# Scores of 192 columns a head pair in place of 256, and the routing's one-hot matrices written by VectorE alone

## The chip, the cores and the metric

The program runs on one core of a Trainium2 chip. The metric is the device time of one execution in microseconds (us); the lower, the better. Engines are named as in the profile: PE (TensorE, with PEld for its weight loads), DVE (VectorE), ACT (ScalarE), POOL (GpSimd), SP (the queue that issues most transfers).

## What is computed

One layer of a small model over 2 x 512 tokens of 256 features, everything in f32: a retention attention and a mixture of experts, both on the layer-normalised input, summed with the residual.

```python
attn = einsum('bhid,bhjd->bhij', q, k) * SCALE            # 16 heads of 16 features
gammas = 1.0 - exp(linspace(log(1/32), log(1/64), H))
dist = arange(S)[:, None] - arange(S)[None, :]
scores = attn * gammas[:, None, None] ** abs(dist) * (dist >= 0)
y = layernorm(einsum('bhij,bhjd->bhid', scores, v)) ; attention = (y * silu(x @ wg.T)) @ wo.T
top_vals, top_idx = top_k(xf @ router_w.T + router_b, 4)   # 32 experts, 4 for each token
rw = softmax(top_vals) * 1.8
routed = sum over the 4 experts of rw * ((silu(x gate_w.T) * (x up_w.T)) @ down_w.T)
shared = (silu(x shared_gate_w.T) * (x shared_up_w.T)) @ shared_down_w.T
out = x + attention + routed + shared
```

## The kernel before

The 1024 tokens are eight tiles of 128 (t = 0 to 7), four to a sequence. Attention goes tile by tile: inside a tile by scores, between tiles by a running state (`from_state`, `chunk_products`, `update_state`). Each engine has its own list of steps in program order, written out by hand, and engines wait for each other by semaphores only. PE's list sets the pace: for each t it has `scores(t)`, transposes of keys and outputs, the projections of tile t+1 (`project_qk`, `project_vg`), `transpose_back(t-2)`, `from_state(t)`, `project_out(t-2)`, `weigh_values(t)`. An output goes through seven hands: PE `weigh_values`, ACT copy, PE transpose, DVE `output_moments`, POOL `output_scale` (four small operations), ACT `normalise_output`, then `gate_output` (three operations of 128 x 256, on POOL or, for tiles 2, 5, 6 and 7, on DVE), then PE `transpose_back` and `project_out`, and DVE `add_residual`. `transpose_keys` for the next tile waits for that residual, since both use one PSUM bank.

**Scores.** The 8 heads of a half g lie in 4 row groups of 32 features (r = 0 to 3), two heads (par = 0, 1) to a row group. ACT makes two copies of the queries with one head of each pair zeroed (`qeo`). One matmul per (g, r) has the 128 keys as weights and the 2 x 128 masked queries as moving columns, so a head pair has 256 columns of scores, of which a quarter (queries of the first 64, keys of the last 64) is zero by the causal mask. The four row groups go to four PSUM banks. DVE's `decay_scores(t, r)` multiplies 512 columns of each bank with the decay table; `weigh_values` multiplies with the values, 16 matmuls of 128 columns, each into its own group of 32 columns of the array.

**Routing.** While attention runs, the choices of experts become slots (`choose_slots`, `assign_slots` at t = 3), and from these two sets of one-hot matrices over 32 groups of choices (a): `pos_hot[a]` (128 x 128, the position in a block) and `blk_code[a]` (128 x 2 x 60, the block, once times a number for (t, k) and once times the token's number). The program makes `pos_hot` by subtraction on ACT (27 of the 32, as |position - column|, at places given by `HOT_STEPS`) and on POOL (`POOL_HOT`, 5 of them), and DVE compares the result with zero, 16 groups at a time (`one_hot_positions`, L1061). DVE makes `blk_hot` (L1064) and its first product (`code_blocks`, L1070), ACT the second (`code_rows`, L597). PE's `route_inverse` (L1422, 32 matmuls) stands behind `scores(6)`; its result becomes `codes` (`make_codes`), with which POOL gathers the tokens of each expert by indirect transfers (L830). The experts then go pair by pair (`transpose_pair` L1553, `gate_up` L1575, `down` L1589), 16 pairs, and the shared expert and the sums end the program.

Of the kernel before, what the change touches and what calls it, by code (L numbers as in the profile page):

```python
# [8 lines left out]
BF16 = mybir.dt.bfloat16  # L9
# [6 lines left out]
P = 128  # L16
# [36 lines left out]
POOL_HOT = range(5, 10)  # L53
HOT_STEPS = {(3, "y"): 5, (4, "z"): 6, (4, "rows"): 2, (5, "tok"): 1, (5, "qk"): 2, (5, "vg"): 11}
HOT_PARTS = 2
# [6 lines left out]
CT = 32  # L62

# [9 lines left out]
C_FILL = C_PI + 1  # L73
# [5 lines left out]


def head_of_slot(s):

    r, g, par = s // 4, s // 2 % 2, s % 2
    return HG * g + 2 * r + par


def constants():
# [13 lines left out]
    c[:, C_PI] = i  # L101
    c[:, C_FILL] = ROWS + P + i
# [7 lines left out]
    dist = i[None, :] - i[:, None]  # L110
    decay = np.zeros((P, H, P))
    for s in range(H):
        decay[:, s] = np.where(dist >= 0, SCALE * gammas[head_of_slot(s)] ** np.maximum(dist, 0), 0.0)
    return c.astype(np.float32), decay.reshape(P, H * P).astype(np.float32)
# [31 lines left out]
def build(nc, x, consts, decay, w_router, w_qkvg, w_out, lnwb, rbias, w_exp, w_late, w_ovf2, w_shared, xn_rows, xnt_rows, y_rows, out):  # L146
    with ExitStack() as ctx:
# [81 lines left out]
        dec = early(H * P)  # L229
        st = early(H * P)  # L230
        qeo = early(2, 2 * KT * P)
# [45 lines left out]
        blk_hot = xb_mem[:, 0:NA * NB // 2].bitcast(BF16).rearrange("p (a b) -> p a b", a=NA)  # L277
# [49 lines left out]
        q_ready = sem("q_ready")  # L327
# [133 lines left out]
        def _(sp):  # L461
# [11 lines left out]
            sp.dma_start(dec[:, 0:H * P // 2], decay[:, 0:H * P // 2]).then_inc(d_in, 16)  # L473
            sp.dma_start(dec[:, H * P // 2:H * P], decay[:, H * P // 2:H * P]).then_inc(c2_in, 16)
# [82 lines left out]
        def _(act):  # L557
# [23 lines left out]

            act_hot = [a for a in range(NA) if a not in POOL_HOT]
            hot = [0]

            def hot_positions(t, place):

                for _ in range(HOT_STEPS.get((t, place), 0)):
                    a = act_hot[hot[0]]
                    if hot[0] == 0:
                        act.wait_ge(pos_sb, 1)  # L590
                    nc.scalar.activation(pos_hot[:, a, :], iota_bf[:, :], ACT.Abs, scale=-1.0, bias=pos_f[:, a:a + 1]
                                         ).then_inc(abs_sb, 1)
                    hot[0] += 1

            def code_rows():
                act.wait_ge(blk_sb, 1)
                nc.scalar.activation(blk_code[:, :, NB:2 * NB], blk_hot[:, :, :], ACT.Copy, scale=cst[:, C_PI:C_PI + 1]  # L597
                                     ).then_inc(rows_sb, 1)

            def take_values_gate(t):  # L600
                act.wait_ge(vg_ps, t + 1)
                nc.scalar.copy(v[:, t % 2, :], ps_vg[:, 0:D]).then_inc(vg_sb, 1)
                if t >= 3:
                    act.wait_ge(z_sb, t - 2)
# [97 lines left out]
            for t in range(NT - 1):  # L702
                if t >= 1:
                    take_output_tokens(t - 1)
                hot_positions(t, "tok")
                take_queries_keys(t + 1)
                hot_positions(t, "qk")
# [5 lines left out]
                hot_positions(t, "z")  # L713
                take_values_gate(t + 1)
                hot_positions(t, "vg")
# [3 lines left out]
                if t == T_RANK + 1:  # L719
                    hot_positions(t, "y")  # L720
                if t == T_RANK + 2:
                    code_rows()
                    hot_positions(t, "rows")
# [52 lines left out]
        def _(pool):  # L776
# [23 lines left out]
            def gate_output(t):  # L800
# [3 lines left out]
                if t == CPB - 1:  # L804
                    pool.wait_ge(z_sb, t)
# [4 lines left out]

            def hot_positions():

                pool.wait_ge(pos_sb, 1)
                pool.wait_ge(pool_cst, 1)
                for a in POOL_HOT:
                    nc.gpsimd.tensor_scalar(pos_hot[:, a, :], iota_bf[:, :], pos_f[:, a:a + 1], None, ALU.subtract
                                            ).then_inc(pool_hot_sb, 1)
# [25 lines left out]
            def spread_values(t):  # L843
# [4 lines left out]
                for par in range(2):  # L848
                    nc.gpsimd.tensor_copy(
                        vz[:, t % 2, :].rearrange("p (h c) -> p h c", c=2 * CT)[:, :, par * 3 * HD:par * 3 * HD + HD],  # L850
                        v[:, t % 2, :].rearrange("p (h d) -> p h d", d=2 * HD)[:, :, par * HD:(par + 1) * HD]
# [5 lines left out]
            step(nc.gpsimd.memset(vz[:, :, :], 0.0))  # L857
# [13 lines left out]
            for t in range(NT):  # L871
# [15 lines left out]
                if t == T_RANK + 1:  # L887
                    hot_positions()
# [1013 lines left out]
```

## Time and profile before

| what | value |
|---|---|
| time, median of 3 runs | 200.25 us (200.07 to 200.26) |
| the profiled execution | 200.26 us, of which the span from the first to the last instruction is 198.4 us |
| PE busy | 190.0 us, 96% of the span |
| DVE, ACT, POOL busy | 117.5, 96.7, 111.8 us |
| granted TensorE clock | 1.00 of 2.4 GHz throughout |
| `scores`, `weigh_values` | L1465 and L1515, once for each of 8 tiles |

A busy share counts every instruction from its start to its end, matmuls by modelled ends, so PE's 96% says that it seldom stood still and not how well it was used. Every f32 matmul is two instructions in the trace. A row of the timeline merges instructions of one line; where an engine stood idle before it, the row ends with how long, and what released it.

### The profile page before, as it was taken

The numbers are of one execution on the slowest core, as the hardware profiler recorded it, in microseconds if no ns is written. First come the engines' busy times: TensorE is split into PE (matmuls) and PEld (weight loads), VectorE is DVE, ScalarE is ACT, GpSimd is POOL, SyncE is SP. The second block draws the span as 40 slices with busy tenths as digits, with TensorE's granted clock in tenths as the row PEclk, the third lists the DMA queues.
The fourth block names the chain that finished last, engine by engine and source line by source line (L and its number), as shares of the span: only waits on it lengthen the run. The fifth ranks groups of instructions, "written<-read, shape, count | busy, mean of one in ns | idle before, by whom it ended". The sixth has DMA issues, their size and how long they took to land.

```text
span 198.4 us, 4872 instructions
## 1 busy us (share of the span) xinstructions
PE 190.0 (96%) x1734; PEld 142.7 (72%) x1734; DVE 117.5 (59%) x360; ACT 96.7 (49%) x242; POOL 111.8 (56%) x156
## 2 busy tenths in 40 slices
PE   8998999999998899899999999999999999999994
PEld 2665756778565667698888678887867877687863
DVE  3478789898897766765632532433342144426894
ACT  3146248555889342653238647734934941123500
POOL 4133057525979468777777677777877743730000
PEclk9999999999999999999999999999999999999999
DMA  4994999998000029999975634324433335229963
GB/s 133 316 374 159 332 403 421 446 444 378 7 0 3 5 56 380 384 358 366 366 288 149 223 106 140 97 90 138 123 104 98 115 91 220 79 82 292 373 262 132
DMA packets 15000, 42.33 MB, mean 213 GB/s; under 512 B 2677, under 2 KB 6138, under 8 KB 14336
## 3 DMA queue, kind: packets, MB, share of 16 engines
q1 hardware_dynamic: 11376, 33.03, 45.5%
q0 software_dynamic: 3456, 8.92, 13.3%
q8 instruction: 14, 0.23, 0.5%
q10 hardware_dynamic: 144, 0.07, 0.2%
q14 instruction: 10, 0.08, 0.1%
HBM read 34.66 MB, written 7.86 MB: 214 GB/s over the span
## 4 chain that ended last, share of the span: by engine, by line
PE 73%; DMA 7%; DVE 7%; issue 4%; POOL 4%; ACT 3%; SPq 0%; ACTq 0%; POOLq 0%; DVEq 0%
PE bank L1575 20%; PE bank L1591 8%; PE bank L1783 5%; PE bank L1589 5%; DMA xg_mem<-xn_rows,codes 4%; PE bank L1440 4%; PE bank L1450 3%; PE bank L1553 3%; DMA w_mem<-w_qkvg_dram 3%; PE bank L1541 3%; PE bank L1612 3%; PE bank L1515 3%; DVE w_mem L1105 2%; PE bank L1465 2%; PE bank L1817 2%
## 5 line engine op out<-in xcount | busy, mean ns | idle before, releaser
L1575 PE MATMUL bank<-xb_mem,w_mem 128*128 128x128 f32 x384 | 47.7, 276 | 0.1
L1575 PEld LDWEIGHTS bank<-xb_mem,w_mem 128*128 128x128 f32 x384 | 45.4, 192 | 0.8 <-issue 0.3
L838 POOL DMA_INDIRECT y_rows<-y_mem,codes x36 | 36.2, 1007 | 16.8 <-issue 9.4
L830 POOL DMA_INDIRECT xg_mem<-xn_rows,codes x36 | 35.4, 984 | 13.0 <-issue 9.7
L1160 DVE TENSOR_TENSOR h_mem<-h_mem,bank 128x128 f32<-128x128 f32 x32 | 9.2, 287 | 42.2 <-ACT h_mem L641 41.9
L1105 DVE TENSOR_TENSOR w_mem<-bank,w_mem 128x512 f32<-128x512 f32 x32 | 20.1, 682 | 2.9 <-PE bank L1465 2.8
L640 ACT ACTIVATE h_mem<-bank 128x128 f32<-128x128 f32 x32 | 8.9, 277 | 23.5 <-PE bank L1575 23.1
L1168 DVE COPY y_mem<-bank 128x256 f32<-128x256 f32 x36 | 15.0, 424 | 7.3 <-PE bank L1591 4.5
L653 ACT COPY w_mem<-w_mem 128x1024 f32 x16 | 16.0, 1042 | 3.2 <-PE bank L1630 2.2
L1591 PE MATMUL bank<-w_mem,h_mem 128*128 128x256 f32 x60 | 17.0, 405 | 0.0
L1440 PE MATMUL bank<-w_mem 128*128 128x128 f32 x128 | 15.9, 278 | 0.2 <-DMA w_mem<-w_qkvg_dram 0.2
L1440 PEld LDWEIGHTS bank<-w_mem 128*128 128x128 f32 x128 | 14.9, 192 | 1.1 <-ACT w_mem L566 0.7
L630 ACT COPY xb_mem<-bank 128x512 f32<-128x512 f32 x16 | 9.4, 585 | 12.6 <-PE bank L1553 12.4
L1450 PE MATMUL bank<-w_mem 128*128 128x512 f32 x32 | 15.1, 593 | 0.0
L1591 PEld LDWEIGHTS bank<-w_mem,h_mem 128*128 128x128 f32 x60 | 10.2, 189 | 5.8 <-issue 5.0
L574 ACT ACTIVATE w_mem<-bank,cst 128x256 f32<-128x256 f32 x16 | 6.7, 470 | 10.0 <-PE bank L1440 10.0
L1783 PE MATMUL bank<-xg_mem,ws_mem 128*128 128x256 f32 x48 | 11.0, 381 | 0.0
L1589 PE MATMUL bank<-w_mem,h_mem 64*128 64x256 f32 x60 | 10.5, 428 | 0.0
L1553 PE MATMUL bank<-cst,xg_mem 128*128 128x128 f32 x64 | 9.7, 275 | 0.7 <-DMA xg_mem<-xn_rows,codes 0.7
L1783 PEld LDWEIGHTS bank<-xg_mem,ws_mem 128*128 128x128 f32 x48 | 9.0, 190 | 1.5 <-DVE h_mem L1292 0.3
L787 POOL TENSOR_TENSOR w_mem<-w_mem,cst 128x256 f32<-128x256 f32 x6 | 5.3, 881 | 8.5 <-ACT w_mem L576 8.5
L1553 PEld LDWEIGHTS bank<-cst,xg_mem 128*128 128x128 f32 x64 | 7.7, 141 | 2.6 <-DMA xg_mem<-xn_rows,codes 0.9
(168 smaller groups left out, 320.7 us busy)
## 6 DMA issues: line engine op xcount, KB each, us to landing
w_mem<-w_exp_dram SPq DMA_DIRECT2D x3, 3456.0 KB, 21.6
w_mem<-w_late_dram SPq DMA_DIRECT2D x7, 1152.0 KB, 8.1
w_mem<-y_rows SPq DMA_DIRECT2D x8, 512.0 KB, 7.3
w_mem<-w_qkvg_dram SPq DMA_DIRECT2D x2, 512.0 KB, 6.3
w_mem<-decay_dram SPq DMA_DIRECT2D x2, 512.0 KB, 7.6
xn_rows<-w_mem SPq DMA_DIRECT2D x2, 512.0 KB, 3.4
xnt_rows<-w_mem SPq DMA_DIRECT2D x1, 1024.0 KB, 4.9
w_mem<-w_ovf_dram SPq DMA_DIRECT2D x16, 64.0 KB
```

What stands on the lines that cost most here:

```text
L653: return nc.scalar.copy(o_mem[:, j * OW:j * OW + XW], w_mem[:, bass.ds(e * EW, XW)])
L830: nc.gpsimd.indirect_dma_start(xg[:, k % RING, :], None, xn_rows, bass.IndirectOffsetOnAxis(ap=codes[:, c, 0:1], axis=0),).then_inc(tok_in ...
L838: nc.gpsimd.indirect_dma_start(y_rows, bass.IndirectOffsetOnAxis(ap=codes[:, c, 1:2], axis=0), ysb[:, k % YRING, :], None, bounds_check=RO ...
L1105: nc.vector.tensor_tensor(st[:, 4 * r * P:4 * (r + 1) * P], ps_s[r][:, :], dec[:, 4 * r * P:4 * (r + 1) * P], ALU.mult).then_inc(sc_sb, 1)
L1168: nc.vector.tensor_copy(ysb[:, w, :], ps[:, 0:D]).then_inc(ys_sb, 1)
L1440: last = nc.tensor.matmul(ps_qk[:, m * P:(m + 1) * P], wqkvg[:, g, m * P:(m + 1) * P], tokens(g, t), start=(g == 0), stop=(g == KT - 1))
L1450: last = nc.tensor.matmul(ps_vg[:, :], tokens(g, t), wqkvg[:, g, 2 * D:4 * D], start=(g == 0), stop=(g == KT - 1))
L1553: last = nc.tensor.transpose(ps_xt[p % 2][:, (2 * g + j) * P:(2 * g + j + 1) * P], xg[:, k % RING, g * P:(g + 1) * P], ident)
L1575: last = nc.tensor.matmul(ps_gu[j][:, m * P:(m + 1) * P], w[:, o:o + P], xbT[:, p % 2, (2 * g + j) * P:(2 * g + j + 1) * P], start=(g == 0 ...
L1589: nc.tensor.matmul(ps_dn[j][:, 0:D], hC[rows, p % 2, :], w2[rows], start=True, stop=False)
L1591: nc.tensor.matmul(ps_dn[j][:, 0:D], hA[:, 2 * (p % 2) + j, :], w[:, j * EW + KT * MB:j * EW + XW], start=False, stop=True).then_inc(dn_ps, 1)
L1783: last = nc.tensor.matmul(to, ws_mem[:, o:o + P], xnT_back[:, g, n], start=(g == 0), stop=(g == KT - 1))
```

## The change

**Scores.** The key tile is cut into halves of 64 keys. ACT now makes two copies of the keys, with the pair's heads interleaved by halves (`keo`): the weights of one matmul are 64 keys of one head beside 64 keys of the other. The first half of the keys meets all 128 queries, the second half only the last 64, so there are two matmuls per (g, r), of 128 and of 64 columns, and a head pair has 192 columns. DVE's `decay_scores` multiplies 384 columns in place of 512; the decay table, st and its transfers shrink by a quarter. `weigh_values` keeps 16 matmuls, eight of 128 columns and eight of 64. The spread values (`vz`) now hold both heads of a pair along the partitions: POOL writes one half by a product with a mask column (L822 after) where it copied before, and ACT writes the other by two copies of 64 x 128 out of PSUM in each `take_values_gate` (L592 after), behind the copy of v and ahead of the gate's Silu.

**Routing.** ACT's 27 and POOL's 5 subtractions, `blk_hot` and `code_rows` are gone. DVE writes each `pos_hot[a]` by one `tensor_scalar` (column number equal to this choice's position, a scalar of each partition), 16 at t = 5 and 16 more at its end, and each `blk_code[a]`'s first half by one `tensor_scalar` with two operations, 32 of 60 columns at t = 4, then the second half of all by one operation of 1920 columns. `gate_output(2)` moves from DVE to POOL.

```diff
     for par in range(2):
-        nc.scalar.activation(qeo[:, t % 2, par * KT * P:(par + 1) * KT * P], ps_qk[:, 0:KT * P], ACT.Copy,
-                             scale=cst[:, C_PM + par:C_PM + par + 1]).then_inc(q_ready, 1)
+        nc.scalar.activation(keo[:, t % 2, :].rearrange("p (a e k) -> p a e k", e=2, k=HF)[:, :, par, :],
+                             ps_qk[:, KT * P:2 * KT * P].rearrange("p (a k) -> p a k", k=HF), ACT.Copy,
+                             scale=cst[:, C_PM + par:C_PM + par + 1]).then_inc(k_ready, 1)
...
     nc.scalar.copy(v[:, t % 2, :], ps_vg[:, 0:D]).then_inc(vg_sb, 1)
+    for half in range(2):
+        par = 1 - half
+        nc.scalar.copy(spread(t, half, par)[par * HF:(par + 1) * HF],
+                       ps_vg[half * HF:(half + 1) * HF, 0:D].rearrange("p (h d) -> p h d", d=CT)
+                       [:, :, par * HD:(par + 1) * HD]).then_inc(vs_sb, 1)
...
 def one_hot_positions(part):
-    a = slice(part * NA // HOT_PARTS, (part + 1) * NA // HOT_PARTS)
-    dve.wait_ge(abs_sb, a.stop - len(POOL_HOT))
-    dve.wait_ge(pool_hot_sb, len(POOL_HOT))
-    nc.vector.tensor_scalar(pos_hot[:, a, :], pos_hot[:, a, :], 0.0, None, ALU.is_equal).then_inc(pos_hot_sb, 1)
+    for a in range(part * NA // 2, (part + 1) * NA // 2):
+        last = nc.vector.tensor_scalar(pos_hot[:, a, :], iota_bf[:, :], pos_f[:, a:a + 1], None, ALU.is_equal)
+    last.then_inc(pos_hot_sb, 1)
...
+def code_blocks():
+    dve.wait_ge(slot_sb, 1)
+    for a in range(NA):
+        last = nc.vector.tensor_scalar(blk_code[:, a, 0:NB], iota_bf[:, 0:NB], blk_f[:, a:a + 1], float(P + a),
+                                       ALU.is_equal, ALU.mult)
+    step(last)
+    nc.vector.tensor_scalar(blk_code[:, :, NB:2 * NB], blk_code[:, :, 0:NB], cst[:, C_PI:C_PI + 1], None,
+                            ALU.min).then_inc(code_sb, 1)
...
-    nc.vector.tensor_tensor(st[:, 4 * r * P:4 * (r + 1) * P], ps_s[r][:, :],
-                            dec[:, 4 * r * P:4 * (r + 1) * P], ALU.mult).then_inc(sc_sb, 1)
+    c = slice(r * KT * PC, (r + 1) * KT * PC)
+    nc.vector.tensor_tensor(st[:, c], ps_s[r][:, 0:KT * PC], dec[:, c], ALU.mult).then_inc(sc_sb, 1)
...
     for g in range(KT):
-        for r in range(HG // 2):
-            rows = slice(CT * r, CT * (r + 1))
-            q = qeo[rows, t % 2, :].rearrange("p (a n) -> p a n", a=2)[:, :, g * P:(g + 1) * P]
-            last = nc.tensor.matmul(ps_s[r][:, 2 * g * P:2 * (g + 1) * P],
-                                    qk[rows, t % 2, (KT + g) * P:(KT + g + 1) * P],
-                                    q, start=True, stop=True)
+        for half in range(2):
+            for r in range(HG // 2):
+                rows, o = slice(CT * r, CT * (r + 1)), g * PC + half * P
+                last = nc.tensor.matmul(ps_s[r][:, o:o + P - half * HF],
+                                        keo[rows, t % 2, (2 * g + half) * P:(2 * g + half + 1) * P],
+                                        qk[rows, t % 2, g * P + half * HF:(g + 1) * P], start=True, stop=True)
```

DVE's list from the scores of tile 4 to those of tile 6, before (L1105 decay, L1142 to L1145 `gate_output(2)`, L1136 residual, L1150 to L1153 moments, L1112 `decay_keys`):

```order
L1105 TENSOR_TENSOR w_mem<-bank,w_mem 128x512 x4
L1142 TENSOR_TENSOR w_mem<-w_mem 128x256
L1143 TENSOR_TENSOR w_mem<-w_mem 128x256
L1145 TENSOR_TENSOR w_mem<-w_mem 128x256
L1064 TENSOR_TENSOR xb_mem<-cst,w_mem 128x1920
L1136 TENSOR_TENSOR x_sb<-x_sb,bank 128x256
...
L1112 TENSOR_TENSOR w_mem<-bank,cst 128x256
L1070 TENSOR_TENSOR h_mem<-xb_mem,cst 128x16x60
L1105 TENSOR_TENSOR w_mem<-bank,w_mem 128x512 x4
...
L1070 TENSOR_TENSOR h_mem<-xb_mem,cst 128x16x60
L1061 TENSOR_SCALAR xg_mem<-xg_mem 128x2048
```

The same place after the change (L1077 decay, L1039 and L1042 `code_blocks`, L1107 residual, L1121 to L1124 moments, L1083 `decay_keys`, L1032 `one_hot_positions`):

```order
L1077 TENSOR_TENSOR w_mem<-bank,w_mem 128x384 x4
L1039 TENSOR_SCALAR h_mem<-w_mem 128x60 x32
L1042 TENSOR_SCALAR h_mem<-h_mem,cst 128x32x60
L1107 TENSOR_TENSOR x_sb<-x_sb,bank 128x256
...
L1083 TENSOR_TENSOR w_mem<-bank,cst 128x256
L1077 TENSOR_TENSOR w_mem<-bank,w_mem 128x384 x4
...
L1032 TENSOR_SCALAR xg_mem<-w_mem 128x128 x16
L1107 TENSOR_TENSOR x_sb<-x_sb,bank 128x256
L1083 TENSOR_TENSOR w_mem<-bank,cst 128x256
L1032 TENSOR_SCALAR xg_mem<-w_mem 128x128 x16
```

The gate of tile 2 has left DVE, all of the block matrices now stand between the decay of tile 4 and the residual of tile 2, and the second half of the position matrices stands directly behind the key decay of tile 5 and ahead of the decay of tile 6, where one compare of 2048 columns stood.

PE's list for one tile's scores after the change (where one row L1465 of 128x256 x8 stood) and its weighing of values (where L1515 of 32x128 x16 stood):

```order
L1430 MATMUL bank<-w_mem 128x128 x4
L1430 MATMUL bank<-w_mem 128x64 x4
L1430 MATMUL bank<-w_mem 128x128 x4
L1430 MATMUL bank<-w_mem 128x64 x4
...
L1480 MATMUL bank<-w_mem 32x128 x4
L1480 MATMUL bank<-w_mem 32x64 x4
L1480 MATMUL bank<-w_mem 32x128 x4
L1480 MATMUL bank<-w_mem 32x64 x4
```

A round of four matmuls (one for each row or column group) of 128 columns alternates with a round of 64; the scores have twice as many matmuls as before, each with weights of its own.

## Rows read from the trace of the kernel before

**Rows 1.** Busy time by stage: the stretch, its length, busy us of each engine (instructions), clock.

```profile
100.00:174.00 74.00, 73.75 (x594) 58.18 (x594) 28.02 (x91) 39.65 (x93) 52.10 (x53) 1.00 0.42 135
```

**Rows 2.** PE's timeline: start us, us, what [idle before it, and its releaser].

```profile
17.95 1.09 PE L1515 MATMUL bank<-w_mem 128*32 128x128 f32 x32 [0.62 <-ACT w_mem L566]
...
34.28 0.27 PE L1403 MATMUL bank<-w_mem 128*128 128x256 bf16 x1 [0.25 <-DVE w_mem L1005]
...
46.23 1.15 PE L1465 MATMUL bank<-w_mem 32*128 32x256 f32 x16
...
51.35 0.44 PE L1532 MATMUL bank<-cst,w_mem 128*128 128x128 f32 x2
...
60.62 0.44 PE L1532 MATMUL bank<-cst,w_mem 128*128 128x128 f32 x2 [0.76 <-POOL w_mem L809]
...
66.10 1.84 PE L1422 MATMUL bank<-h_mem,xg_mem 128*128 128x120 bf16 x32 [0.94 <-DVE xg_mem L1061]
...
84.41 0.63 PE L1553 MATMUL bank<-cst,xg_mem 128*128 128x128 f32 x4 [0.69 <-DMA xg_mem<-xn_rows,codes]
```

**Rows 3.** The chain that ended last, in order of time: start us, us, what.

```profile
51.79 1.02 PE bank L1515 x32
...
76.15 7.62 DMA xg_mem<-xn_rows,codes
...
117.66 0.43 PE bank L1630 x8
```

**Rows 4.** Busy time of L1465 alone, scores of tile 6: PE and PEld (instructions running).

```profile
64.01:64.11 0.10, 0.10 (x4) 0.10 (x4) 1.00 0.00 0
64.11:64.33 0.22, 0.22 (x4) 0.21 (x8) 1.00 0.00 0
```

**Rows 5.** DVE's timeline, as rows 2.

```profile
14.58 1.48 DVE L945 TENSOR_SCALAR w_mem<-x_sb,w_mem 128x256 f32<-128x256 f32 x4
15.98 1.87 DVE L1105 TENSOR_TENSOR w_mem<-bank,w_mem 128x512 f32<-128x512 f32 x3
...
23.87 0.83 DVE L986 MAX8 w_mem<-w_mem 128x8 f32<-128x32 f32 x8
...
46.37 0.14 DVE L1153 TENSOR_SCALAR w_mem<-w_mem 128x1 f32<-128x1 f32 x1
...
47.39 2.49 DVE L1105 TENSOR_TENSOR w_mem<-bank,w_mem 128x512 f32<-128x512 f32 x4 [0.55 <-PE bank L1465]
...
53.91 0.42 DVE L1136 TENSOR_TENSOR x_sb<-x_sb,bank 128x256 f32<-128x256 f32 x1 [0.54 <-PE bank L1541]
...
54.99 0.14 DVE L1153 TENSOR_SCALAR w_mem<-w_mem 128x1 f32<-128x1 f32 x1
...
60.09 1.50 DVE L1070 TENSOR_TENSOR h_mem<-xb_mem,cst 128x960 bf16<-128x960 bf16 x1
61.51 1.22 DVE L1061 TENSOR_SCALAR xg_mem<-xg_mem 128x2048 bf16<-128x2048 bf16 x1
...
65.26 0.69 DVE L1061 TENSOR_SCALAR xg_mem<-xg_mem 128x2048 bf16<-128x2048 bf16 x1 [0.71 <-ACT xg_mem L591]
```

**Rows 6.** Groups by shape, of DVE and ACT: busy us, mean ns of one.

```profile
L1105 DVE TENSOR_TENSOR w_mem<-bank,w_mem 128x512 f32<-128x512 f32 x32 | 20.1, 682 | 2.9 <-PE bank L1465 2.8
...
L641 ACT ACTIVATE h_mem<-bank 64x128 f32<-64x128 f32 x32 | 8.7, 273 | 0.8
...
L1112 DVE TENSOR_TENSOR w_mem<-bank,cst 128x256 f32<-128x256 f32 x6 | 2.5, 425 | 3.8 <-PE bank L1478 3.8
```

**Rows 7.** POOL's timeline, as rows 2.

```profile
48.26 0.53 POOL L849 COPY w_mem<-w_mem 128x128 f32<-128x128 f32 x2
...
55.89 1.16 POOL L795 TENSOR_SCALAR w_mem<-w_mem 128x1 f32<-128x1 f32 x1
...
60.53 1.64 POOL L787 TENSOR_TENSOR w_mem<-w_mem,cst 128x256 f32<-128x256 f32 x1
...
63.24 0.34 POOL L795 TENSOR_SCALAR w_mem<-w_mem 128x1 f32<-128x1 f32 x1
...
75.25 0.73 POOL L787 TENSOR_TENSOR w_mem<-w_mem,cst 128x256 f32<-128x256 f32 x1
```

More of the change, by code:

```diff
@@ L62 @@
 CT = 32
+HF = P // 2
+PC = P + HF
+ST = H // 2 * PC
 C_ID = 0
@@ L72 @@
 C_PI = C_IO + P
-C_FILL = C_PI + 1
+C_HF = C_PI + 1
+C_FILL = C_HF + 2
 C_TK = C_FILL + 1
@@ L101, in constants @@
     c[:, C_PI] = i
+    for half in range(2):
+        c[:, C_HF + half] = i // HF == half
     c[:, C_FILL] = ROWS + P + i
@@ L109, in constants @@
     c[:, C_ED:C_ED + E] = E * P - P - P * e[None, :]
[L110 to L114, printed above, removed]
+    decay = np.zeros((P, HG // 2, KT, PC))
+    query = np.concatenate([i, i[HF:]])
+    key = i[:, None] % HF + np.where(np.arange(PC) < P, 0, HF)[None, :]
+    dist = query[None, :] - key
+    for r in range(HG // 2):
+        for g in range(KT):
+            gamma = gammas[HG * g + 2 * r + i // HF][:, None]
+            decay[:, r, g] = np.where(dist >= 0, SCALE * gamma ** np.maximum(dist, 0), 0.0)
+    return c.astype(np.float32), decay.reshape(P, ST).astype(np.float32)
 def token_blocks():
@@ L431, in state_reads, with spread @@
             return sum(1 for u in range(t + 1) if u % CPB > 0)
+        def spread(t, half, par):
+            return vz[:, t % 2, half * D:(half + 1) * D].rearrange("p (h c) -> p h c", c=CT)[:, :, par * HD:(par + 1) * HD]
         def need(eng, semaphore, value):
@@ L580, in take_logits_transposed @@
                 nc.scalar.copy(lgT[:, :], ps_vg[:, 0:2 * P]).then_inc(lgT_sb, 1)
[L582 to L598, printed above, removed]
             def take_values_gate(t):
@@ L886, in _ @@
                     spread_values(t + 1)
-                if t == T_RANK + 1:
-                    hot_positions()
-                if 1 <= t < NT - 2 and t != CPB - 1:
+                if 1 <= t < NT - 2:
                     gate_output(t - 1)
@@ L1240, in _ @@
                 if t == T_RANK + 2:
-                    gate_output(CPB - 2)
-                    dve.wait_ge(pos_sb, 1)
-                    one_hot_blocks()
+                    code_blocks()
                     add_residual(t - 2)
@@ L1252, in _ @@
                 if t == T_RANK + 3:
-                    code_blocks(1)
                     one_hot_positions(0)
@@ L1262, in _ @@
                     decay_keys(t)
-                if t == T_RANK + 2:
-                    code_blocks(0)
                 if t == T_RANK - 1:
@@ L1509, in weigh_values @@
                 pe.wait_ge(vz_sb, 2 * (t + 1))
+                pe.wait_ge(vs_sb, 2 * (t + 1))
                 for g in range(KT):
-                    for par in range(2):
+                    for half in range(2):
                         for r in range(HG // 2):
-                            s = 4 * r + 2 * g + par
-                            h = head_of_slot(s)
-                            last = nc.tensor.matmul(ps_y[CT * r:CT * (r + 1), g * P:(g + 1) * P],
-                                                    vz[:, t % 2, h * CT:(h + 1) * CT], st[:, s * P:(s + 1) * P],
-                                                    start=(g == 0 and par == 0 and t % CPB == 0),
-                                                    stop=(par == 1), skip_group_check=True)
+                            o = (KT * r + g) * PC + half * P
+                            last = nc.tensor.matmul(ps_y[CT * r:CT * (r + 1), g * P + half * HF:(g + 1) * P],
+                                                    vz[:, t % 2, half * D + g * P + CT * r:half * D + g * P + CT * (r + 1)],
+                                                    st[:, o:o + P - half * HF],
+                                                    start=(g == 0 and half == 0 and t % CPB == 0),
+                                                    stop=(half == 1), skip_group_check=True)
                 last.then_inc(y_ps, 1)
```

86 lines of the change are left out of this document (28 added, 58 removed).

## The prediction

> **What bounds the kernel now.** I read the windows by stage first. While the experts run PE is busy 73.75 of 74 us [rows 1], and nothing there is changed: what the change is worth must be decided before, and the experts begin later or earlier by that much. PE's timeline gives the waits ahead of them [rows 2]: 0.62 at 17.95, 0.25 at 34.28, 0.76 at 60.62 (the gated output of tile 3), 0.94 at 66.10, where `route_inverse` waits for DVE's compare of the position matrices, and 0.69 at 84.41 for gathered tokens. The chain of waits joins the last two: the gather that ends last runs from 76.15 for 7.62 [rows 3], and it was issued from the codes that `route_inverse` yields. From 66.10 to 84.41 are 18.3 us in which no operation on that path changes (DVE's decays of tile 6 lie beside PE's 1.84 of inverse). What PE saves in tiles 6 and 7 only lengthens the wait of 0.69. So the shift of `route_inverse`, 66.10 now, is the shift of the end. The profiled execution took 200.26 (span 198.4, 1.86 around it), the median is 200.25; I sum against 200.26.
>
> **PE's part.** Four column groups run beside each other: 8 instructions of 256 columns take 0.43 [rows 3], two rounds of 0.213, 0.83 ns a column. `weigh_values` has eight rounds of 128 columns (0.107 each, 0.85 of its 1.02) [rows 3]; after, four have 64 columns: -0.21 a tile.
>
> The scores are another matter. In [rows 4] the first 0.10 goes to four weight loads of 128 columns; then the next four loads already run beside the first matmuls (x8 against x4), and a round takes 0.22, its 256 columns. Before: 0.10 + 4 x 0.215 = 0.96. After there are eight rounds, each with new weights of 128 columns; a round of 64 columns (0.053) can't pass to the next before that one's loads (0.10 to 0.107) are in. So 0.10 + 7 x 0.107 + 0.053 = 0.90: -0.05 a tile. By columns alone it would be 0.10 + 4 x 0.107 + 4 x 0.053 = 0.74, -0.22. I take -0.05; the bounds are 0 and -0.22.
>
> The Trainium skill, "TensorE: Matmul & The Clock Gate", section "Part 3: Packing small matmuls — row/col tiling", says that a weight load overlaps matmuls in flight only in other row groups, which would speak against the change. By that each round would pay load and matmul, 1.28 before and 1.50 after, +0.22 a tile. [rows 4] shows the loads beside matmuls of the same four groups, so the trace disagrees.
>
> **Up to the scores of tile 4 (46.23).** The wait at 17.95 is put down to ACT, whose copy was done at 17.5; DVE's three decays end at 17.85 [rows 5], and that is the true releaser. A decay of 512 columns takes 682 ns and one of 256 columns 425 [rows 6], 1.0 ns a column, so 384 columns save 0.13: three save 0.39. The wait at 34.28 is for a DVE chain with four decays in it (-0.5), so it goes: 0.25. With four `weigh_values` (0.84) and four scores (0.20) tile 4 starts 1.7 earlier. DVE's decay of it starts at 45.7 (47.39 now [rows 5]) and takes 1.95 for 2.49: 47.65.
>
> ACT's two new copies (0.27 each by its 64-partition row [rows 6], 0.55 a tile) are hidden: ACT loses 27 subtractions, and `take_outputs` behind them waits for PE. Uncovered, 0.55 would come at each tile. POOL's spread (0.53 the pair [rows 7]; as a product over two inputs half of a 128x256 product, 0.37 each) lies beside ACT's normalising. `gate_output(2)` on POOL costs three products, 2.2. DVE's moments of tile 2 end at 46.51 [rows 5], 44.8 with 1.7 off, and the path from moments to a gated output (4.67, below) gives 49.5; PE's L1532 takes it at 51.35 [rows 2], 49.65 with 1.7 off. It adds nothing, but its cover is 0.15.
>
> **The one-hot matrices.** Two prices are unknown: one `tensor_scalar` with a scalar of each partition, and what DVE and POOL cost each other. Small DVE operations follow each other at about 0.10 for 32 columns (eight in 0.83) [rows 5], so 0.065 fixed. On bf16 with a constant scalar 2048 columns take 0.69 [rows 5], four columns a ns; on f32 with two scalars of each partition 256 columns take 0.37 (four in 1.48) [rows 5], one a ns. The new operations are bf16 like the first and have partition scalars like the second. Per operation of 60 and 128 columns that is 0.08 and 0.10, or 0.13 and 0.19; the last operation of 1920 columns 0.65 or 2.0. I take the first, nearest in type.
>
> That has a price. In [rows 5, 7] DVE and POOL take turns: DVE's 1.50 to 61.59, POOL's product issued at 60.53 takes 1.64 for 0.73, DVE's compare issued at 61.51 takes 1.22 for 0.69. Each stands still for the operation of the other that is in progress. So fast operations wait for POOL's and POOL for them, and 65 of them meet that.
>
> `code_blocks`: 32 x 0.08 + 0.65 = 3.25, with POOL's last two gate products and one `decay_queries` (3 x 0.7) between: 5.3, in place of the gate and one product of 3.6. Behind it are queued residual and moments (1.22, from 53.91 to 55.13 [rows 5]): 47.65 + 5.3 + 1.22 = 54.2. From the moments to `transpose_back(3)` are now 60.62 - 55.13 = 5.49, of which 0.82 was one POOL operation that stood behind DVE (1.16 for 0.34 [rows 7]): 4.67, and 0.2 for new handovers. So 59.05, and the wait at 60.62 shrinks.
>
> From there PE needs 66.10 - 60.62 - 0.94 = 4.54 to the inverse; its key transposes end 1.1 before that and `weigh_values` gives 0.21: 3.2. DVE's key decay 0.5, then 16 operations 1.6, a handover 0.1: 64.45 if POOL is out of the way. But POOL gates tile 4 just then, 2.2: 66.65 if DVE stands behind all of it. Midway is 65.5, 0.6 before 66.10. **Forecast: 200.26 - 0.6 = 199.6**, a slight gain: DVE takes ACT's place as the one that `route_inverse` waits for.
>
> **Rivals.**
> (1) Partition scalars run a column a ns, without turns. `code_blocks` 32 x 0.13 + 2.0 = 6.15: moments end 55.0, `transpose_back(3)` 59.7, inverse 59.7 + 3.8 + 3.1 = 66.6: +0.5, 200.8. For it: the f32 row. Against it: that row is not bf16.
> The Trainium skill, "VectorE: DVE Perf Modes", section "The perf-mode tier table", gives `tensor_scalar` 4x on bf16 and 2x on f32, with no exception for partition scalars. The f32 row ran at 1x, so the trace disagrees there, which feeds this rival; what bf16 with such a scalar does no row shows.
> (2) Slower by the port: POOL always goes first. Moments of tile 4 are done at 57.9 (54.2, key decay 0.5, decay of tile 5 1.95, running sums 0.2, moments 1.0). From there POOL has about 6.1 of work (rest of a gate 1.1, `decay_queries` 0.7, `output_scale` four times 0.34, spread 0.75, gate 4 2.2) and DVE 32 operations, 3.2; in a row they end at 67.2: +1.1, 201.4. It decides once DVE gets less than one operation in per POOL operation.
> (3) Faster: no turns are lost. `code_blocks` ends before PE's `project_out(2)`, the residual starts near 51.95 (53.91 less 1.7 and what tile 4 saves, 0.26), moments end 53.2, `transpose_back(3)` 57.8, inverse 57.8 + 3.8 + 1.6 = 63.2: -2.9, 197.4. For it: the operations are short, and ACT and POOL lose all their subtractions.
> (4) Loads don't overlap matmuls: +0.27 a tile against my sum, 1.1 up to tile 4, all passed on: 200.7. [rows 4] speaks against it.
>
> **How the numbers follow.** Chances: forecast 0.42, (1) 0.25, (2) 0.14, (3) 0.14, (4) 0.05. The forecast's own range is 64.45 to 66.65, 198.6 to 200.8. The overall range cuts into (3) and (2): 197.8 to 201.2. A change of 0.2%, 0.4 us, is about what a measurement here can tell from none. Faster by more: most of (3), 0.6 of the forecast, a little of (1), 0.44. Within: 0.3 of the forecast, 0.45 of (1) and a little else, 0.27. Slower: 0.29.
>
> **What would show it.** Right: scores near 1.0 a tile, `weigh_values` 0.80; tile 4's scores near 44.5; the position operations at 0.10 apart but with gaps of POOL's length; `route_inverse` waiting over 1 us for DVE; the gather as late behind the codes as now. Wrong: operations 0.19 apart; `route_inverse` waiting for nothing; ACT's copies ahead of a PE wait; a gated tile 2 later than 49.65.

## The result, and the profile after

The changed kernel takes 206.25 us (median of 4 runs, 204.98 to 207.31) where the kernel before takes 200.25: 1.030 of its time, interval 1.023 to 1.036. The profiled execution took 206.82, with a span of 205.0. Forecast were 199.6 and a range up to 201.2, so even the sign is wrong. Medians below are over all runs of a kernel; ratios leave out runs more than 1.5% above the kernel's fastest.

The experts are no slower, they only begin later. Busy time by stage, as in [rows 1] (the columns are PE, PEld, DVE, ACT, POOL, the clock, the DMA share):

```profile
100.00:174.00 74.00, 73.98 (x606) 59.39 (x606) 28.87 (x92) 40.77 (x96) 52.91 (x54) 1.00 0.48 160
```

PE's timeline, to be held against [rows 2]:

```profile
17.93 0.88 PE L1480 MATMUL bank<-w_mem 128*32 128x128 f32 x32 [0.49 <-ACT w_mem L568]
...
36.87 1.12 PE L1430 MATMUL bank<-w_mem 32*128 32x128 f32 x32
38.05 0.33 PE L1453 MATMUL bank<-w_mem 128*32 128x32 f32 x14
39.98 0.31 PE L1453 MATMUL bank<-w_mem 128*32 128x32 f32 x2 [1.61 <-issue]
40.23 0.69 PE L1490 MATMUL bank<-cst,w_mem 128*128 128x128 f32 x2
40.71 3.18 PE L1405 MATMUL bank<-w_mem 128*128 128x128 f32 x16
...
48.19 1.12 PE L1430 MATMUL bank<-w_mem 32*128 32x128 f32 x32
...
57.72 0.44 PE L1443 MATMUL bank<-cst,w_mem 128*128 128x128 f32 x2 [1.40 <-DVE x_sb L1107]
...
63.10 0.44 PE L1498 MATMUL bank<-cst,w_mem 128*128 128x128 f32 x2 [0.21 <-POOL w_mem L790]
...
66.81 1.12 PE L1430 MATMUL bank<-w_mem 32*128 32x128 f32 x32
71.03 3.23 PE L1387 MATMUL bank<-h_mem,xg_mem 128*128 128x120 bf16 x32 [3.11 <-DVE xg_mem L1032]
74.19 0.33 PE L1453 MATMUL bank<-w_mem 128*32 128x32 f32 x16
```

Three things are to be seen. First, PE stands for 1.61 us in the middle of `chunk_products` (L1453), after 14 of its 16 instructions, and "issue" says that nothing in the profile released it. What follows (L1405) takes 3.18 for the 1.95 to 2.05 of the other tiles. Second, PE waits for the residual behind `code_blocks` at 57.72. Third, `route_inverse` (L1387) waits 3.11 for the position matrices and then takes 3.23 where it took 1.84 [rows 2]. It starts 4.93 later than before and what follows it starts 6.3 later; the end came 6.6 later (205.0 for 198.4).

The granted clock, microsecond by microsecond, says why L1405 and L1387 were long:

```profile
41.00:42.00 1.00, 1.00 (x7) 1.00 (x7) 1.00 (x2) 0.33 (x1) 0.00 (x0) 0.50 1.03 442
...
44.00:45.00 1.00, 1.00 (x3) 0.38 (x2) 0.90 (x6) 1.00 (x3) 0.00 (x0) 1.00 1.03 442
...
72.00:73.00 1.00, 1.00 (x13) 1.00 (x12) 0.28 (x1) 0.00 (x0) 0.00 (x0) 0.50 0.00 0
...
74.00:75.00 1.00, 1.00 (x24) 0.81 (x23) 0.63 (x3) 0.07 (x1) 0.00 (x0) 1.00 0.00 0
```

At 41 and at 72 it is 0.50 (1.2 GHz), behind the two gaps, and some 3 us later 1.00 again (2.4 GHz). In the trace of before it was 1.00 in every stage up to the experts.

DVE's timeline, to be held against [rows 5]:

```profile
49.33 1.95 DVE L1077 TENSOR_TENSOR w_mem<-bank,w_mem 128x384 f32<-128x384 f32 x4 [1.42 <-PE bank L1430]
51.20 5.38 DVE L1039 TENSOR_SCALAR h_mem<-w_mem 128x60 bf16<-128x60 bf16 x32
56.62 0.72 DVE L1042 TENSOR_SCALAR h_mem<-h_mem,cst 128x1920 bf16<-128x1920 bf16 x1
57.25 0.41 DVE L1107 TENSOR_TENSOR x_sb<-x_sb,bank 128x256 f32<-128x256 f32 x1
...
58.33 0.14 DVE L1124 TENSOR_SCALAR w_mem<-w_mem 128x1 f32<-128x1 f32 x1
...
62.00 4.05 DVE L1032 TENSOR_SCALAR xg_mem<-w_mem 128x128 bf16<-128x128 bf16 x16
65.97 0.41 DVE L1107 TENSOR_TENSOR x_sb<-x_sb,bank 128x256 f32<-128x256 f32 x1
66.91 0.42 DVE L1083 TENSOR_TENSOR w_mem<-bank,cst 128x256 f32<-128x256 f32 x1 [0.53 <-PE bank L1443]
67.25 3.63 DVE L1032 TENSOR_SCALAR xg_mem<-w_mem 128x128 bf16<-128x128 bf16 x16
```

From 51.2 to 70.8 DVE hardly rests: 6.05 for the block matrices (51.20 to 57.25) and 7.7 for the two sets of position matrices. Before, a gate and the block compare took 3.6 ahead of the residual at 53.91, two products behind it 1.15 and 1.50, and the two compares 1.2 and 0.7 (the last three in [rows 5], the others in the same trace).

### The profile page after: what moved, and what is told of

The parts are those of the page before. It is cut to its first block, busy times and chain, and to the rows that moved or that the text cites. A ratio compares the mean times of both kernels' runs of the same rounds, so it can differ in the third digit from the quotient of the medians.

```text
span 205.0 us, 5167 instructions
## 1 busy us (share of the span) xinstructions
PE 191.6 (93%) x1862; PEld 147.4 (72%) x1862; DVE 118.8 (58%) x417; ACT 92.3 (45%) x230; POOL 109.0 (53%) x154
## 4 chain that ended last, share of the span: by engine, by line
PE 76%; DVE 12%; POOL 4%; issue 4%; ACT 2%; ACTq 0%; POOLq 0%
PE bank L1541 21%; PE bank L1557 8%; PE bank L1749 5%; PE bank L1405 5%; PE bank L1555 5%; PE bank L1415 4%; DVE xg_mem L1032 4%; PE bank L1328 3%; PE bank L1578 3%; PE bank L1519 3%; DVE h_mem L1039 3%; PE bank L1783 2%; PE bank L1430 2%; POOL xg_mem L803 2%; PE bank L1507 2%
## 5 line engine op out<-in xcount | busy, mean ns | idle before, releaser
L1077 DVE TENSOR_TENSOR w_mem<-bank,w_mem 128x384 f32<-128x384 f32 x32 | 15.8, 547 | 3.3 <-PE bank L1430 3.3
L1405 PE MATMUL bank<-w_mem 128*128 128x128 f32 x128 | 17.2, 291 | 0.0
L1405 PEld LDWEIGHTS bank<-w_mem 128*128 128x128 f32 x128 | 16.2, 206 | 0.5 <-ACT w_mem L568 0.3
L777 POOL TENSOR_TENSOR w_mem<-w_mem 128x1 f32<-128x1 f32 x8 | 4.6, 572 | 11.0 <-DVE w_mem L1124 11.0
L1281 DVE SCALAR_TENSOR_TENSOR x_sb<-w_mem,rw,x_sb 128x256 f32<-128x256 f32 x22 | 9.5, 478 | 0.2
```

The costliest lines, as they stand in the source:

```text
L1077: nc.vector.tensor_tensor(st[:, c], ps_s[r][:, 0:KT * PC], dec[:, c], ALU.mult).then_inc(sc_sb, 1)
L1405: last = nc.tensor.matmul(ps_qk[:, m * P:(m + 1) * P], wqkvg[:, g, m * P:(m + 1) * P], tokens(g, t), start=(g == 0), stop=(g == KT - 1))
```

## The experiments

Two theories stood against each other at first: that the scores part lost the time (a longer PE list that runs dry), or the routing part (DVE operations dearer than I took them).

**1. The scores part alone.** All hunks of keys, scores, decay and values; the routing of before.

> The scores part alone: scores of 192 columns, keys copied twice, values spread by ACT and POOL; the routing's matrices made as before. First theory (the stall belongs to the longer PE list): a tile has 32 more PE instructions, PE's fourth instruction block comes from memory late because the queues are full of expert weights (DMA share 1.00), so PE stands for about 1.8 us in chunk_products at tile 3 with no releaser, then the clock is at 0.50 for about 3 us; scores of tile 4 near 48, end about 1.5 to 2.5 us later than before, 201.5 to 203. Rival (the stall comes with the routing's edit, or by chance): no such gap, scores of tile 4 near 45.1, 199.0 to 200.0.

Measured: 202.07 (10 runs, 200.48 to 203.78; kernel before on the same chip 200.54), ratio 1.007, interval 1.004 to 1.010. The gap is there at the same instruction, shorter, and the inverse waits:

```profile
39.27 0.25 PE L1508 MATMUL bank<-w_mem 128*32 128x32 f32 x2 [0.78 <-issue]
...
66.91 2.47 PE L1442 MATMUL bank<-h_mem,xg_mem 128*128 128x120 bf16 x32 [1.89 <-DVE xg_mem L1081]
```

The gap belongs to the scores part. ACT's last 11 absolute differences, in this run and in the kernel before:

```profile
62.73 3.31 ACT L602 ACTIVATE xg_mem<-w_mem 128x128 bf16<-128x128 bf16 x11
```
```profile
61.91 3.32 ACT L591 ACTIVATE xg_mem<-w_mem 128x128 bf16<-128x128 bf16 x11
```

They begin 0.8 later, behind the two new copies (0.56), and the compare behind them releases the inverse: the cover that I gave those copies is gone. The granted clock did not fall behind the gap at tile 3, but it fell during the inverse, which takes 2.47 for 1.84.

**2. The routing part alone.** The other hunks; scores of 256 columns.

> The routing part alone: one-hot matrices by DVE, gate of tile 2 on POOL; scores, decays and values as before. If the routing's price is its own: scores of tile 4 at 46.2 as before, code blocks 6.0 on DVE, residual of tile 2 at 55.9 in place of 53.9, 16 position operations of about 3.6 ahead of the inverse, which then starts near 69.5 with PE idle for 2.5 or more ahead of it and runs at a clock of 0.50 (3.2 in place of 1.84): 204 to 205.5. Rival (the routing costs only because the scores part came late): inverse within 1 us of 66.1, 200 to 201.5.

Measured: 206.83 (205.82 to 207.17), ratio 1.030, interval 1.027 to 1.033. By itself it costs all that the whole change costs. No gap at tile 3; DVE and PE:

```profile
50.05 6.11 DVE L1019 TENSOR_SCALAR h_mem<-w_mem 128x60 bf16<-128x60 bf16 x32
...
61.63 3.68 DVE L1012 TENSOR_SCALAR xg_mem<-w_mem 128x128 bf16<-128x128 bf16 x16
...
67.42 3.85 DVE L1012 TENSOR_SCALAR xg_mem<-w_mem 128x128 bf16<-128x128 bf16 x16
```
```profile
57.31 0.44 PE L1423 MATMUL bank<-cst,w_mem 128*128 128x128 f32 x2 [2.29 <-DVE x_sb L1087]
...
58.81 3.27 PE L1385 MATMUL bank<-w_mem 128*128 128x128 f32 x16
...
71.41 3.19 PE L1367 MATMUL bank<-h_mem,xg_mem 128*128 128x120 bf16 x32 [3.30 <-DVE xg_mem L1012]
```

The inverse is 5.3 late and runs at half clock; it came 1.9 later than this run's expectation had it. The block matrices took 6.8 in place of 6.0 (POOL's gate of tile 2 lies beside them here), the second set 3.85 in place of 3.6, and the clock was at 0.50 also behind the wait of 2.29 for the residual, so that the projection at 58.81 took 3.27 for 2.05.

**3. Queues empty at the gap.** The loads of expert weights wait for the scores of tile 4:

```diff
+            sp.wait_ge(sc_ps, 20)
             for p in range(0, EARLY, BATCH_IN):
```

> The changed kernel with one wait added on SP: the three loads of expert weights start only after the scores of tile 4, so the queues are nearly empty from 28 to 45 us; all else is the same. Theory (PE's instruction block was late because of the full queues): the gap of 1.8 us at tile 3 and the half clock behind it are gone, scores of tile 4 near 45.2, 2.4 to 3.0 us off: 203 to 204, and the spread of the runs shrinks. Rival (the gap is at a place of PE's list, whatever the queues do): the gap stays, 206 to 207.

Measured: 205.31 (203.42 to 206.86), ratio 1.022, interval 1.014 to 1.031; against 1.030 the intervals overlap. The same 4 us of the changed kernel and of this one:

```profile
36.00:40.00 4.00, 2.22 (x70) 1.65 (x59) 3.85 (x8) 1.08 (x3) 2.86 (x5) 0.98 0.97 412
```
```profile
36.00:40.00 4.00, 3.83 (x92) 3.33 (x85) 3.89 (x9) 1.61 (x4) 2.86 (x5) 1.00 0.02 4
```

With the DMA share at 0.02 in place of 0.97 PE is busy 3.83 in place of 2.22: the gap is gone, and scores of tile 4 start at 44.99. The spread did not shrink as expected. The runs' mean clocks say why: 203.42 and 204.26 at 0.992, 206.36 and 206.86 at 0.967. A stretch of 3.4 us at half clock, as the two in the trace of the changed kernel are, lowers a mean over 203 us by 0.0084 (an estimate), so these are one and four such stretches; the changed kernel's runs have 0.992 to 0.975.

The records of PE's instruction transfers (queue q8 of the profile; 15 packets of 16 KB for 3,870 records of PE in the changed kernel, so some 256 instructions each) stand behind the gap. Instructions are counted from the first record; the last column has when PE began the 961st and when it began the next one:

```
kernel                 fetch of the block    961st / next
before                 39.97 to 40.92        45.57 / 45.58
changed                37.58 to 38.57        38.17 / 39.98
scores part alone      36.96 to 37.99        38.29 / 39.27
changed, late weights  34.31 to 35.27        38.30 / 38.31
```

Sixteen more matmul instructions a tile, each with its load, bring PE to the 961st instruction 7 us sooner, and with full queues the block comes too late for it: it lands 0.4 behind the 961st instruction in the changed kernel and 0.3 ahead of it in run 1, and in both PE goes on only 1.4 and 1.3 behind its landing. The Trainium skill, "Runtime: NRT & Kernel Launch", section "Instruction fetch mechanics", describes blocks of 16 KiB that each engine fetches by a queue of its own, with a crossing mostly hidden; the size agrees with the packets here, and the 1.61 shows a crossing that wasn't hidden.

**4. The price of one operation.** Series of 12 DVE operations behind the last sum of the kernel before, results unused, in one execution:

```diff
+            series("ptr bf16 128", 12, lambda i: nc.vector.tensor_scalar(
+                o16[:, i, 0:P], bf_iota, point(i), None, ALU.is_equal))
+            series("const bf16 128", 12, lambda i: nc.vector.tensor_scalar(
+                o16[:, i, 0:P], bf_iota, float(i), None, ALU.is_equal))
...
```

> The kernel before with series of 12 DVE operations behind its last sum, whose results go nowhere: tensor_scalar on bf16 with a scalar of each partition and with a constant, of 128 and of 60 columns, the same on f32, from f32 to bf16, and two products over broadcast inputs of 1024 columns. The changed kernel's pitch was 0.163 for 128 and 0.146 for 60 columns. First theory (the scalar of each partition costs the extra fixed time): with a constant 0.10 and 0.08. Second theory (the fast bf16 form itself has a fixed time of 0.13): 0.163 and 0.146 with a constant too, and on f32 about 0.20 or less for 128.

```profile
196.65 2.04 DVE L1368 TENSOR_SCALAR h_mem<-xb_mem,cst 128x128 bf16<-128x128 bf16 x12
198.73 1.32 DVE L1370 TENSOR_SCALAR h_mem<-xb_mem 128x128 bf16<-128x128 bf16 x12
200.08 1.84 DVE L1372 TENSOR_SCALAR h_mem<-xb_mem,cst 128x60 bf16<-128x60 bf16 x12
201.95 1.11 DVE L1374 TENSOR_SCALAR h_mem<-xb_mem 128x60 bf16<-128x60 bf16 x12
203.10 2.44 DVE L1376 TENSOR_SCALAR h_mem<-cst 128x128 f32<-128x128 f32 x12
205.58 1.72 DVE L1378 TENSOR_SCALAR h_mem<-cst 128x128 f32<-128x128 f32 x12
```

Rows with `cst` among the inputs have a scalar of each partition, the others a constant. The difference is 0.72 of 12, 0.73 and 0.72: **a scalar of each partition costs 0.060 an operation**, for both types and both widths. The columns run at the same rate with either: between 128 and 60 columns lie 0.017 (0.20 of 12), four columns a ns. f32 takes 0.033 more than bf16 for 128 columns, with either scalar, which is half of bf16's rate if the fixed time is the same.

**5. PE kept busy in its waits.** On top of the late weights, matmuls without a reader:

```diff
                 if t == CPB + 1:
+                    warm_up(8, ps_qk)
                     transpose_keys(CPB)
...
                 if t == T_INVERT:
+                    warm_up(12, ps_qk)
                     route_inverse()
```

> The changed kernel with the late weights and with matmuls on PE whose results nobody reads, ahead of two of its waits: 8 of 512 columns ahead of the key transposes of tile 4, 12 ahead of the inverse. DVE, ACT and POOL have the same lists, so the inverse starts no earlier (DVE's last position operation sets it). Theory (part of the loss is the half clock that PE gets after it has stood still): the inverse takes 1.84 in place of 3.2, the clock is 1.00 throughout, 1.4 off the fastest runs with late weights, 201.6 to 202.4, with the runs within 1 us of each other. Rival (the granted clock does not follow what PE did): inverse 3.2, 203.4 to 206.9 as without them.

Measured: 202.46 (202.30 to 202.97, 6 runs), ratio 1.010, interval 1.007 to 1.013, mean clock 0.999 to 1.000 in each run.

```profile
67.97 1.84 PE L1388 MATMUL bank<-h_mem,xg_mem 128*128 128x120 bf16 x32 [0.71 <-DVE xg_mem L1033]
```

The inverse is back at 1.84, and the spread of 3.4 has become 0.7. So late block and half clock together are 3.8 of the 6.0 (206.25 - 202.46). About 2 remain: the inverse comes 1.9 later than before (67.97 for 66.10) and waits for DVE's positions. This is net of what the shorter scores save, so the DVE operations cost more than that by themselves, and 202.46 still lies beyond the forecast's range (201.2).

**6. The scores part with late weights.** The wait of run 3 in the kernel of run 1.

> The scores part alone with the late weights. Theory (the scores part loses by PE's late instruction block): no gap at tile 3, scores of tile 4 near 45.0, inverse at 66.0 to 66.9, since ACT's absolute differences, behind its two new copies of each tile, then end last: 200.0 to 201.0. Rival (ACT's copies alone make it slow): inverse at 66.9 and later, 201.5 to 202.5 as without the late weights.

Measured: 201.49 (13 runs, 200.07 to 207.16), ratio 1.0025, interval 1.0004 to 1.0046. The gap at tile 3 is gone, but the inverse still waits 1.89 for the compare behind ACT, at 65.78. Its profiled execution was the longest of the runs, with a wait of 4.38 at 113 that the kernel before does not have; nothing of its experts is read from it.

**7. The position matrices divided anew.** As run 6, ACT with 19 and DVE with 8 of ACT's 27, in a place where DVE stood still:

```diff
-HOT_STEPS = {..., (5, "vg"): 11}
+HOT_STEPS = {..., (5, "vg"): 3}
+DVE_HOT = range(24, 32)
...
+            def one_hot_direct():
+                for a in DVE_HOT:
+                    last = nc.vector.tensor_scalar(pos_hot[:, a, :], iota_bf[:, :], pos_f[:, a:a + 1], None, ALU.is_equal)
...
                     one_hot_positions(0)
+                    one_hot_direct()
```

> The scores part with late weights, and the position matrices divided anew: ACT makes 19 in place of 27 by absolute difference, and DVE makes the 8 last ones with one operation each, right behind its first compare, where it stood still for 1.6. Theory (DVE at 0.163 an operation is fine where it has room, and ACT was the last ahead of the inverse): ACT ends 2.4 earlier, the inverse is released by PE's own scores or by the compare at 65.0 to 65.8, 198.8 to 199.8, under the kernel before. Rival (DVE's operations delay POOL's gate of tile 3 and so PE's transpose of it): no gain over the late weights alone.

Measured: 201.43 (12 runs, 200.20 to 203.66), ratio 1.004, interval 1.001 to 1.007: a miss in time, and no gain over run 6, though the inverse did what was said.

```profile
63.59 1.85 PE L1450 MATMUL bank<-h_mem,xg_mem 128*128 128x120 bf16 x32
...
66.23 0.26 PE L1516 MATMUL bank<-w_mem 128*32 128x32 f32 x4 [0.55 <-issue]
...
83.08 0.63 PE L1582 MATMUL bank<-cst,xg_mem 128*128 128x128 f32 x4 [1.18 <-issue]
...
109.49 1.58 PE L1604 MATMUL bank<-xb_mem,w_mem 128*128 128x128 f32 x12 [1.89 <-DVE h_mem L1189]
```

It waits for nobody and starts 2.5 before the kernel before. Gaps of 3.6 follow, where the kernel before has 0.69 at 84.41 [rows 2], and give that back. The first is a late block again: behind the 1729th instruction, with the queues full (DMA share 0.98 from 60 to 64), PE goes on 1.4 behind the landing at 64.82.

**8. The new division in the kernel before.**

> The kernel before with the same new division of the position matrices alone (old scores, weights not held back). Theory: inverse's wait of 0.94 goes, 0.5 to 0.9 under the kernel before, 199.4 to 199.9. Rival (8 more DVE operations hold up POOL's products): same as before or slower, 200.2 to 200.8.

Measured: 200.48, ratio 0.9997, interval 0.998 to 1.001: no difference, as the rival had it. In the profiled execution the inverse waits 0.20, not 0.94, but PE had waited 0.72 for the residual just before, which 8 operations of DVE now precede.

**9. A shorter hold.** Run 7 with `sc_ps, 16`, so that the loads start at 38.3.

> As the scores part with late weights and the new division of the position matrices, but the expert weights wait only for the scores of tile 3 (37.9) in place of tile 4 (45). In that kernel the inverse started at 63.6, 2.5 before the kernel before, and was given back by PE's late block at 65.5 (0.55), by the first gathered tokens (1.2 at 83) and by 1.9 at 109, where PE waited with the third batch of experts. Theory (these three come from weights that still load when codes, gathers and late weights begin): with loads done 7 us earlier they shrink, the end comes 1.5 to 2.5 before the kernel before, 198.0 to 199.0. Rival (the later stages have limits of their own, whatever the inverse does): 200.0 to 201.0.

Measured: **198.75** (198.43 to 200.03), ratio 0.9925, interval 0.990 to 0.995: faster than both kernels. All waits that PE's timeline shows from 30 to 112:

```profile
54.00 0.44 PE L1553 MATMUL bank<-cst,w_mem 128*128 128x128 f32 x2 [0.45 <-ACT w_mem L633]
...
59.79 0.44 PE L1561 MATMUL bank<-cst,w_mem 128*128 128x128 f32 x2 [1.40 <-POOL w_mem L829]
...
66.96 0.26 PE L1516 MATMUL bank<-w_mem 128*32 128x32 f32 x4 [0.83 <-issue]
```

The waits at 83 and 109 have gone with the earlier loads. A late block remains behind the 1729th instruction, three blocks behind the 961st (landing at 65.64, DMA share 0.99 from 60 to 64).

**10. The block matrices alone**, with the gate of tile 2 on POOL, and **11. the position matrices alone**, both in the kernel before.

> Of the routing part only the block matrices (32 operations of 60 columns and one of 1920 on DVE, gate of tile 2 on POOL); position matrices by ACT and POOL, scores as before. DVE then has 6.1 to 6.8 between the decay of tile 4 and the residual of tile 2 where it had 4.1. Theory (the block matrices push the whole chain by their own excess): residual at 56.4 to 56.9, transpose of tile 3 near 63.4, inverse 2.3 to 3.2 later than before, with a half clock there in some runs: 202.5 to 204.5. Rival (the positions cost nearly all): 200.3 to 201.3.

> Of the routing part only the position matrices (two times 16 operations of 128 columns on DVE), block matrices as before, nothing on ACT and POOL for positions. At 0.163 each and about 1 of turns with POOL each set takes 3.6 to 4.0; the second set stands between the key decay of tile 5 and the inverse, where a compare of 0.69 stood. Theory: inverse 2 to 3 later than before, PE idle there for 2.5 to 3.5 and its clock at half in most runs: 202.5 to 204.5; block matrices and positions then add up to what the routing part costs (6.3). Rival (POOL freed of five subtractions of 5.06 gives it back): 200.3 to 201.3.

Measured: 203.85 (ratio 1.017, interval 1.014 to 1.019) and 205.44 (1.024, 1.022 to 1.027), the second above its range. Neither rival holds, but the two don't add up to the routing part either: 3.2 and 4.8 against 6.3. In run 10 DVE took 7.5 for the block matrices and the inverse starts at 69.51; but there POOL still makes its five subtractions ahead of the gate of tile 2, and PE waited 2.62 for that gate:

```profile
54.10 0.44 PE L1528 MATMUL bank<-cst,w_mem 128*128 128x128 f32 x2 [2.62 <-POOL w_mem L806]
```
```profile
58.15 0.42 DVE L1137 TENSOR_TENSOR x_sb<-x_sb,bank 128x256 f32<-128x256 f32 x1 [0.57 <-PE bank L1537]
```

DVE's residual behind the matrices waited 0.57 for PE and not for them, so the 3.2 is not their price: what they cost by themselves this run does not show. In run 11 the inverse starts at 69.35, at half clock:

```profile
69.35 3.36 PE L1419 MATMUL bank<-h_mem,xg_mem 128*128 128x120 bf16 x32 [2.64 <-DVE xg_mem L1057]
```

**12. The hold in the kernel before**, as the control.

> The kernel before with the expert weights held back until the scores of tile 3, all else the same: the control for the kernels with held weights. PE has no late instruction block before the experts in the trace of before, so nothing is to be gained: 200.0 to 200.6. If the weights come too late for the experts, a wait near 109 and 201 or more.

Measured: 200.83, ratio 1.0004, interval 0.999 to 1.002: nothing, as expected. So neither the hold nor the new division (run 8) gains anything in the kernel before, and with the shorter scores hold and division together do (run 9). Whether all three are needed is not shown: no run has the shorter scores with the division and no hold, or with the shorter hold and the old division.

## Why the prediction was wrong

**The price of the one-hot operations** is the first of the steps that failed; the routing part costs 3% even by itself (run 2). "Per operation of 60 and 128 columns that is 0.08 and 0.10, or 0.13 and 0.19 ... I take the first" chose the rate rightly, and both choices had the wrong fixed time. I took 0.065 from operations without a scalar of each partition; with one it is 0.13, which run 4 shows (operations of 128 columns begin 0.163 apart, of which the columns are 0.032; 2.04 for 12 against 1.32 with a constant). 64 operations times 0.060 are 3.8, and all 64 stand ahead of the inverse in the list of the engine that it waits for. The f32 row that I read as one column a ns is two columns a ns and two scalars: inside it the operations begin 0.32 apart (15.01, 15.33, 15.65; the 0.37 has a longer first one in it), and run 4's prices give 0.07 + 0.13 + 2 x 0.06 = 0.32. With that, the Trainium skill's "VectorE: DVE Perf Modes", section "The perf-mode tier table", which I had said the trace contradicts for f32, agrees with run 4: f32 with such a scalar is as fast a column as with a constant.

**The turns with POOL** were too large for the block matrices and too small for the positions. I had put 2 into 5.3; POOL did one operation beside them after 51.5 and then stood still until 58.5, for it waits for the moments behind them. The 6.05 are the operations nearly alone (32 at 0.15 and 0.7 are 5.6), and that they came within 0.75 of the 5.3 is luck: a price too low and turns too many. The two sets of positions took 4.05 and 3.63, of which 16 at 0.17 (2.04 / 12) are 2.7: 1.3 and 0.9 went in turns. In the first set the operations at 62.46 and 63.01 are 0.55 and 0.69 from the next, beside POOL's products at 62.40 and 63.00; in the second set two are 0.55 from the next, again beside POOL's products. I had only the second set on the path, at 1.6; the first delays the residual of tile 3 too, to 65.97 where PE's product was done at 65.2.

**"Tile 4 starts 1.7 earlier"** failed by a term that wasn't there, and in the profiled execution it is the largest. Up to the scores of tile 3 PE gained 1.27 (36.87 for 38.14). Then the late instruction block and the half clock behind it cost 3.45 between these scores and the gate projection of the next tile (6.85 for 3.40), and tile 4 started 1.96 later. Counting 16 more matmuls a tile as PE time alone was the mistake. The 0.4 at 17.95 hardly came either: the three decays got shorter, but the small DVE operations ahead of them ended later (15.00 for 14.58), and the wait went from 0.62 to 0.49.

**The half clock at the inverse**, 1.39, had no term either, though the forecast had PE wait over 1 us there. Run 5 shows the price by taking it away.

By these steps the inverse: 65.5 forecast, + 3.55 (DVE's decay of tile 4 ends at 51.20 and not 47.65) + 0.75 (6.05 for 5.3) - 0.25 (the steps to the transpose of tile 3) + 1.5 (from there to the inverse 7.93 for 6.45) = 71.0; + 1.39 for its clock, and 0.3 behind it, is the difference of 7.2 between 199.6 and 206.82. (A slip in the recorded sum, 32 x 0.08 + 0.65 = 3.25 for 3.21, changes nothing.)

**What was right:** `weigh_values` 0.88 for 1.09 (-0.21), scores 1.12 for 1.15 (-0.03, forecast -0.05). Their rounds are those of the weight loads: in the windows of the scores of tile 6 each round of four takes 0.10 to 0.11, with eight loads and up to 16 matmuls running,

```profile
67.13:67.23 0.10, 0.10 (x16) 0.10 (x8) 1.00 0.00 0
67.23:67.34 0.11, 0.11 (x16) 0.11 (x8) 1.00 0.00 0
```

so rival (4) fell. Of the other rivals, (2) comes nearest by its number, with 67.2 for the inverse, but only two or three of the 16 operations of a set stood behind a product of POOL's; (1), with 66.6, is right that a scalar of each partition makes the operation dearer, but by a rate that run 4 denies. None had the inverse later than 67.2. The path from moments to a gated output held (4.71 for 4.87). The rule that the shift of the inverse is the shift of the end held only with the half clock added: 4.93 and 1.39 and 0.3 are the 6.6. And it holds for a late inverse; run 7 had it 2.5 earlier without an earlier end. ACT's copies came ahead of a wait of PE only with the old routing (run 1).

**Open:** how much of the 3.8 of run 5 is the late block and how much the clock in a typical run, since run 3's interval overlaps with the changed kernel's; what DVE's operations cost in the changed kernel by themselves (runs 10 and 11 do not separate the two sets); and what sets the delay of a block: it came 3.3 us behind PE's 705th instruction with idle queues (30.97 to 34.31) and 6.8 behind it with full ones (30.82 to 37.58).

## What to carry to other kernels

Price a small operation by the nearest row with the same operands, not the same type: many small operations are their fixed time, and a scalar of each partition is part of that. More matmuls are also more instructions to fetch; where the transfer queues are full, look for gaps that nothing released (1.61 in the middle of a line here). And a wait of PE of two or three microseconds can cost more than itself, when the clock is at half behind it (the inverse took 3.23 for 1.84): put work there, or move work from the engine that is waited for to one that stands still.

## What the runs showed of the hardware that was not expected

- On DVE a scalar of each partition adds 0.060 to a `tensor_scalar`, for bf16 of 60 and of 128 columns and f32 of 128 alike (run 4).
- PE can stand still in the middle of a line of independent matmuls, 0.6 to 1.6 us, when its next block of 256 instructions lands late (behind the 961st instruction in the changed kernel and run 1, behind the 1729th in runs 7 and 9). In all four PE went on 1.3 to 1.4 us behind the end of the block's packet.
- The granted clock fell to 0.50 behind gaps of 1.61 and 3.11 us in the changed kernel and was at 1.00 again some 3 us later; behind the gap of 0.78 in run 1 it did not fall. The length of the gap alone does not decide it: it fell behind a wait of 1.89 in run 1 and not behind one of 1.89 in run 7. It also differs from run to run: the mean clock of the changed kernel's four runs was 0.975 to 0.992.
